# A pre-norm attention and FFN layer on one core: first weight columns in three groups, the next input split inside its step, another order in step 1

## The chip, the core and the metric

The kernel runs on one core of a Trainium2 chip. The metric is the device time of one execution in microseconds (us), lower is better. The kernel before was run three times.

## What is computed

x is 8 batches of 512 rows of 256, all fp32. Attention with 16 heads of 64 reads a layer norm followed by an RMS norm of x, and its projected output is added to x; an FFN (256 to 1024 to 256, GELU) with a per-row router weight reads a layer norm of that and is added too.

```python
def rms_norm(x, gamma):
    norm = jnp.maximum(jnp.linalg.norm(x, axis=-1, keepdims=True), eps)
    return x / norm * x.shape[-1] ** 0.5 * (gamma + 1.0)
qkv = rms_norm(layernorm(x), gamma) @ w_qkv      # 256 x 3072
attn = jax.nn.softmax((q * scale) @ k.T)         # 8 batches, 16 heads, 512 x 512
x = x + (attn @ v) @ w_out
out = gelu(xt @ w1 + b1) @ w2 + b2
x = x + out * jnp.sum(combine, axis=-1, keepdims=True)
```

## The kernel before

Every product keeps fp32 accuracy by a split: an operand is held as a rounded **high part** (fp32r) and a **low part** (the value less its high part), and `products` (L449) multiplies high by high, low by high and high by low, so each block of one output costs six matmuls (two halves of K by three terms). So every intermediate that TensorE (PE) will read again is read twice out of PSUM: once by ScalarE (ACT), which writes the high part, then by VectorE (DVE), which subtracts and writes the low part (`lo`, L925). Weights are staged in SBUF and split the same way; their low parts are made by GpSimd (POOL, L871) or VectorE.

The attention work is a hand-written software pipeline. A *unit* n is one pair of heads and one tile of 128 query rows; there are 256. A *step* holds units 2*step and 2*step+1, and 16 steps are one batch. In step s, PE does, in this order (L645 to L665):

1. the transposes of the probabilities of unit 2s-3 (`transpose_prob`, L476, into banks 4 and 5),
2. the scores of units 2s and 2s+1 (`scores`, L457),
3. the transposes of unit 2s-2 (banks 6 and 7),
4. "aux" blocks of place 1 (bank 4), the weighted values of step s-2 (`weighted_values`, L502, bank 5), and aux blocks of places 2 and 3 (banks 6 and 7).

Aux blocks are what `plan_aux` (L75) lays out: `xt` (the normalised input transposed, two blocks per batch), `q`, `k` and `v` products of the next heads, and `out` (the output projection). VectorE takes for each unit the row maxima out of PSUM (`row_max`, L993), ScalarE the exponentials (`exp`, L737), VectorE the inverse of the row sums (L1000), and POOL scales the probabilities (`normalise_prob`, L839). ScalarE and VectorE then make the high and low parts of the transposed probabilities (`transposed_hi`, L726; `transposed_lo`, L982). High and low parts of aux blocks of places 2 and 3 are made at the *start of the following step* (L773 and L1056). The exponentials write into three buffers `prob`, so unit n's may start only when unit n-3 has been transposed. At the very start `prob`, `wstage` and `halves_out` hold staged weights, so the first units also wait for these to be split (L742).

Steps -10 to -1 are the lead-in. SyncE issues the loads of x, then 128 columns each of the q and k weights (`first_stage`, L307), then six chunks of the remaining qkv weights (L281 to L286). Each chunk is split at a *slot* (half a step) of the table L301:

```python
POOL_CHUNKS = (0, 2, 3, 4, 5, 6, 7)
slot_of_chunks = {-12: [0], -9: [1], -8: [2], -6: [3], -5: [4], -4: [5], 6: [6], 10: [7]}
```

Until its operands are there PE runs matmuls on zeros (`keep_warm`, L640; counts in `WARM`, L58). The first batch's transposed input is made in steps -4 and -3, q and k of the first two heads in step -3, and step 0 starts with their scores. Later batches' `xt` blocks are issued at the end of step 13 of each batch (rel == 13, L95), in banks 6 and 7. PE's next transposes into these banks (unit 2s-2, L490) wait until both have their low parts.

## Time and profile before

| | us |
|---|---|
| median of 3 runs | 1218.33 |
| lowest, highest | 1218.26, 1219.44 |
| the profiled execution | 1219.89 |
| its span in the trace | 1218.0 |

The profiled execution's time has 1.9 us around its span. Times in the trace count from the span's start. Steps 0 to 127 lie between 19 and about 1000 us, with the FFN behind them.

### The profile page before, as it was taken

What the parts mean: (1) busy time and instruction counts of PE and PEld (TensorE: products, weight loads), DVE (VectorE), ACT (ScalarE), POOL (GpSimd) and SP (SyncE); (2) the same over time, 40 slices, a digit from 0 to 9 for tenths busy, and PEclk for the clock granted to TensorE, in tenths of its full rate; (3) what the DMA queues carried; (4) which work ended last, traced back from release to release, by engine and by line L of the source; (5) the groups of instructions that cost most, each with busy time, mean ns of one, the idle gap of its engine ahead of it and who ended that gap; (6) DMA issues with size and microseconds to landing.
All of it is one profiled execution on the core that took longest, in us unless ns stands there. A gap on an engine that the chain in (4) does not pass through costs nothing. (4 is left out here: it accounts for less than half of the span.)

```text
span 1218.0 us, 29275 instructions
## 1 busy us (share of the span) xinstructions
PE 1189.3 (98%) x11355; PEld 1041.3 (85%) x11355; DVE 962.4 (79%) x1739; ACT 894.0 (73%) x1926; POOL 640.3 (53%) x797
## 2 busy tenths in 40 slices
PE   7999999999999999999999999999999989999998
PEld 5878888888888888888888888888888878888887
DVE  5788788877887788878887897889788987666644
ACT  5788888888888888788878888888788884334432
POOL 5565555555565555556555565556555654322221
PEclk9999999999999999999999999999999999999999
DMA  4122111311131113111311131113111222111100
GB/s 158 36 53 71 36 36 37 87 36 36 36 88 36 37 36 87 36 37 36 88 36 36 37 87 37 36 36 87 36 36 36 71 77 85 35 48 57 36 18 36
DMA packets 32633, 62.92 MB, mean 52 GB/s; under 512 B 5744, under 2 KB 9072, under 8 KB 32496
## 3 DMA queue, kind: packets, MB, share of 16 engines
q1 hardware_dynamic: 32496, 61.05, 19.5%
q8 instruction: 92, 1.51, 0.5%
q14 instruction: 45, 0.37, 0.1%
HBM read 19.08 MB, written 8.39 MB: 23 GB/s over the span
## 5 line engine op out<-in xcount | busy, mean ns | idle before, releaser
L827 POOL TENSOR_SCALAR prob<-prob,rowinv 128x512 f32<-128x512 f32 x512 | 350.5, 699 | 313.3 <-DVE rowinv L1000 310.1
L744 ACT ACTIVATE prob<-ps,negmax 128x512 f32<-128x512 f32 x512 | 347.1, 686 | 36.8 <-DVE negmax L995 32.8
L927 DVE TENSOR_TENSOR pT_lo<-ps,pT_hi 128x512 fp32r<-128x512 f32 (+1 forms) x384 | 320.3, 862 | 24.9 <-ACT pT_hi L735 18.8
L995 DVE TENSOR_REDUCE negmax<-ps 128x2 f32<-128x1024 f32 x256 | 310.9, 1215 | 1.1 <-PE ps L473 1.1
L497 PEld LDWEIGHTS ps<-identity,prob 64*128 64x128 f32 x4096 | 154.0, 139 | 71.3 <-issue 33.4
L732 ACT ACTIVATE pT_hi<-ps 128x1024 fp32r<-128x1024 f32 x128 | 131.5, 1027 | 104.4 <-issue 101.5
L497 PE MATMUL ps<-identity,prob 64*128 64x64 f32 x4096 | 177.8, 226 | 13.0 <-POOL prob L827 10.2
L469 PE MATMUL ps<-nat 64*128 64x512 f32 x1024 | 171.7, 411 | 1.4 <-DVE nat L927 1.4
L511 PE MATMUL ps<-pT_hi,vbuf 128*128 128x256 f32 x1024 | 164.3, 282 | 3.0 <-DVE pT_lo L927 3.0
L511 PE MATMUL ps<-pT_lo,vbuf 128*128 128x256 f32 x1024 | 164.0, 282 | 0.0
L511 PEld LDWEIGHTS ps<-pT_hi,vbuf 128*128 128x128 f32 x1024 | 144.1, 189 | 9.9 <-DVE pT_lo L927 4.2
L735 ACT ACTIVATE pT_hi<-ps 128x512 fp32r<-128x512 f32 x256 | 140.5, 610 | 16.4 <-PE ps L497 16.4
L511 PEld LDWEIGHTS ps<-pT_lo,vbuf 128*128 128x128 f32 x1024 | 140.6, 190 | 0.0
L453 PE MATMUL ps<-xT_hi,wbig_hi 128*128 128x512 f32 x320 | 133.1, 416 | 2.4 <-DVE xT_lo L928 2.4
L847 POOL TENSOR_TENSOR att_hi_v<-att_hi_v,att_lo_v 128x512 f32<-128x512 f32 x64 | 83.4, 1302 | 91.6 <-DMA att_lo_v<-halves_out 91.6
L1000 DVE RECIPROCAL rowinv<-rowsum 128x2 f32<-128x2 f32 x256 | 40.9, 160 | 112.6 <-ACT prob L744 112.3
L453 PE MATMUL ps<-xT_hi,wbig_lo 128*128 128x512 f32 x320 | 127.5, 398 | 0.0
L453 PE MATMUL ps<-xT_lo,wbig_hi 128*128 128x512 f32 x320 | 125.5, 392 | 0.0
L744 ACT ACTIVATION_READ_ACCUMULATOR prob<-ps,negmax 128x1 f32 x512 | 102.9, 201 | 0.0
L473 PE MATMUL ps<-nat 64*128 64x512 f32 x512 | 102.0, 393 | 0.0
L469 PEld LDWEIGHTS ps<-nat 64*128 64x128 f32 x1024 | 88.1, 188 | 14.0 <-DVE nat L927 1.9
L836 POOL TENSOR_SCALAR pT_hi<-prob 128x512 fp32r<-128x512 f32 x64 | 41.0, 643 | 102.8 <-ACT prob L761 102.8
(116 smaller groups left out, 2317.0 us busy)
## 6 DMA issues: line engine op xcount, KB each, us to landing
att_hi_v<-halves_out SPq DMA_DIRECT2D x128, 128.0 KB, 2.3
att_lo_v<-halves_out SPq DMA_DIRECT2D x128, 128.0 KB, 2.4
xres<-in_x SPq DMA_DIRECT2D x8, 512.0 KB, 3.5
x_scratch<-xres SPq DMA_DIRECT2D x8, 512.0 KB, 2.9
out_y<-f_o SPq DMA_DIRECT2D x16, 256.0 KB, 2.0
xin<-in_x SPq DMA_DIRECT2D x7, 512.0 KB, 4.2
wstage<-in_w SPq DMA_DIRECT2D x4, 512.0 KB, 3.8
xin<-x_scratch SPq DMA_DIRECT2D x3, 512.0 KB, 3.8
```

What stands on the lines that cost most here:

```text
L453: ins = pe.matmul(dst, stationary[i], moving[j], start=first and n == 0, stop=last and n == len(terms) - 1)
L469: pe.matmul(ps[:, PS_SCORE[n % 2] + h, :], part[rows, q_part, q0:q0 + P], part[rows, k_part, :], start=q_part == QH, stop=False)
L473: pe.matmul(ps[:, PS_SCORE[n % 2] + h, :], part[rows, QH, q0:q0 + P], part[rows, KL, :], start=False, stop=True).then_inc(s_score, 1)
L497: ins = pe.transpose(ps[:, bank + r, a * DH:(a + 1) * DH], prob[rows, n % NPROB, a * P:(a + 1) * P], identity[rows, rows])
L511: ins = pe.matmul(ps[:, PS_OUT, h * 2 * P:(h + 1) * 2 * P], vbuf[:, quad % 2, k, pair % 2 * 2 + h, :], pT[part][:, t % 2, h * TT + k, :], ...
L732: act.activation(even_tile(n)[0], two_bank_blocks(PS_PT_EVEN), ACT.Copy).then_inc(s_pthi, 2)
L735: act.activation(odd_tiles(n)[r][0], bank_blocks(PS_PT_ODD + r), ACT.Copy).then_inc(s_pthi, 1)
L744: act.activation(prob[:, n % NPROB, j * SEQ:(j + 1) * SEQ], ps[:, PS_SCORE[n % 2] + j, :], ACT.Exp, bias=negmax[:, n % 4, j:j + 1], accum_ ...
L827: return pool.tensor_scalar(dst, src, scalar, 1.0, ALU.mult, ALU.mult)
L847: pool.tensor_tensor(att_hi_v[:, :], att_hi_v[:, :], att_lo_v[:, :], ALU.add).then_inc(s_head, 1)
L927: return dve.tensor_tensor(dst, full, hi, ALU.subtract)
L995: dve.tensor_reduce(negmax[:, n % 4, :], ps[:, PS_SCORE[n % 2]:PS_SCORE[n % 2] + 2, :], AX.X, ALU.max, negate=True).then_inc(s_max, 1)
```

## The change

**First columns in three groups.** Beside the 128 q and k columns of the first pair of heads (group 0), the same of the second pair (group 1) and 256 v columns (group 2) are loaded in pieces of their own, into `att_lo_v` and `xres`, ahead of the six chunks, which are 768 wide now. ScalarE makes the high parts of the three in slots -17 to -15, VectorE the low part of group 0, POOL those of groups 1 and 2 once the normalised input is there. The chunks are split later (0 and 1 behind the first input's high parts, 2 in step -2, 3, 4 and 5 in steps 0, 1 and 2), all low parts by POOL.

**Around the first products.** k comes before q; each half of K waits for its own half of the input. The first query tile (128 columns) has its high and low part made first, and unit 0's scores wait for it alone. `gain` is computed behind the normalisation. Three and one fewer matmuls on zeros. The second half of the first v block moves from step 1 to step 0 (place 4, bank 5).

**Step 1.** VectorE takes both row maxima and ScalarE the exponentials of unit 2 before unit 0's transposed parts.

**The next batch's input.** In step 13 of each batch ScalarE makes the high part of the first `xt` block inside the step, ahead of the second exponentials; for batches 1 to 7 VectorE makes the high part of the second block itself (`input_hi`) and then both low parts, at the end of the step. For the FFN's first input (behind batch 7) ScalarE makes both high parts there.

**POOL.** The layer norm's powers (`powers`) come behind `normalise_prob` of the odd unit instead of ahead of it.

The diff's core:

```diff
-WARM = {FIRST_STEP: 22, -3: 5}
+WARM = {FIRST_STEP: 19, -3: 4}
-PS_AUX = {1: 4, 2: 6, 3: 7}
+PS_AUX = {1: 4, 2: 6, 3: 7, 4: 5}
...
-            blocks += [(1, "q", 0), (2, "k", 0)]
+            blocks += [(1, "k", 0), (2, "q", 0)]
         if step == 0:
-            blocks.append((3, "v", 0, 0))
+            blocks += [(3, "v", 0, 0), (4, "v", 0, 1)]
...
-        POOL_CHUNKS = (0, 2, 3, 4, 5, 6, 7)
-        slot_of_chunks = {-12: [0], -9: [1], -8: [2], -6: [3], -5: [4], -4: [5], 6: [6], 10: [7]}
+        POOL_CHUNKS = (0, 1, 2, 3, 4, 5, 6, 7)
+        slot_of_chunks = {-6: [0, 1], -4: [2], 1: [3], 3: [4], 5: [5], 6: [6], 10: [7]}
...
+            for k in range(KT):
+                sp.dma_start(first_stage[1][:, k], first_source[1][:, k]).then_inc(s_first_load[1], 16)
+            for k in range(KT):
+                sp.dma_start(first_stage[2][:, k], first_source[2][:, k]).then_inc(s_first_load[2], 16)
             for i in range(7):
                 load_weight(sp, i)
...
+                if n == 0:
+                    pe.wait_ge(s_q_first, 1)
+                if n == 1:
+                    pe.wait_ge(s_aux, aux_index[("q", 0)] + 1)
...
+                if n == 1:
+                    pe.wait_ge(s_aux, aux_index[("v", 0, 1)] + 1)
...
+                    start = P if pair == 0 else 0
+                    if start:
+                        act.activation(nat[:, 0, QH, 0:start], bank[:, 0:start], ACT.Copy, scale=SCALE)\
+                            .then_inc(s_q_first_hi, 1)
+                        act.wait_ge(s_q_first, 1)
...
-                for block_of_aux in aux_of(step - 1)[1]:
+                for block_of_aux in late_blocks(step - 1):
                     aux_hi(*block_of_aux)
...
-                if 0 <= 2 * step - 2 < NUNIT:
+                if 0 <= 2 * step - 2 < NUNIT and step != 1:
                     transposed_hi(2 * step - 2)
                 if 0 <= 2 * step < NUNIT:
                     exp(2 * step)
+                if step == 1:
+                    transposed_hi(0)
...
                     copy_halves(step - 2)
+                for block_of_aux in turned_blocks(step):
+                    aux_hi(*block_of_aux)
                 if 0 <= 2 * step + 1 < NUNIT:
                     exp(2 * step + 1)
...
+            def input_hi(block_no, place, kind, b, k):
+                dve.wait_ge(s_auxfull, block_no + 1)
+                link(dve.tensor_scalar(xT[0][:, k, :], ps[:, aux_bank(block_no), :], gain[:, k:k + 1], None, ALU.mult))
...
                 slot_tasks(2 * step + 1)
+                for block_of_aux in turned_blocks(step):
+                    if split_by_vector(*block_of_aux[2:]):
+                        input_hi(*block_of_aux)
+                for block_of_aux in turned_blocks(step):
+                    aux_done(*block_of_aux)
```

**ScalarE at the start**, before (`wbig_hi` is the high part of the qkv weights, `xT_hi` that of the transposed input, `nat` holds q and k):

```order
L767 ACTIVATE wbig_hi<-att_hi_v 128x2x2x128 [waits first_columns_loaded]
L770 ACTIVATE wbig_hi<-prob 128x896 [waits weights_loaded0]
L770 ACTIVATE wbig_hi<-prob 128x896 [waits weights_loaded1]
L770 ACTIVATE wbig_hi<-prob 128x896 [waits weights_loaded2]
L703 ACTIVATE xT_hi<-ps,gain 128x512 [waits aux_block_in_psum] x2
L770 ACTIVATE wbig_hi<-wstage 128x896 [waits weights_loaded3]
L708 ACTIVATE nat<-ps 128x512 [waits aux_block_in_psum]
```

and now:

```order
L812 ACTIVATE wbig_hi<-att_hi_v 128x2x2x128 [waits first_columns_loaded0]
L812 ACTIVATE wbig_hi<-att_lo_v 128x2x2x128 [waits first_columns_loaded1]
L812 ACTIVATE wbig_hi<-xres 128x2x256 [waits first_columns_loaded2]
L740 ACTIVATE xT_hi<-ps,gain 128x512 [waits gain_ready,aux_block_in_psum] x2
L815 ACTIVATE wbig_hi<-prob 128x768 [waits weights_loaded0]
L815 ACTIVATE wbig_hi<-prob 128x768 [waits weights_loaded1]
L753 ACTIVATE nat<-ps 128x512 [waits aux_block_in_psum]
L747 ACTIVATE nat<-ps 128x128 [waits aux_block_in_psum]
L750 ACTIVATE nat<-ps 128x384 [waits first_query_tile_done]
```

The input's high parts stand ahead of every whole chunk, and behind the two small groups.

**ScalarE in steps 1 and 2** now (the first row is the exponential of unit 2, `halves_out` here stages chunk 4):

```order
L786 ACTIVATE prob,rowsum<-ps,negmax 128x512 [waits weights_lo_pool,rowmax_done]
L786 ACTIVATE prob,rowsum<-ps,negmax 128x512
L774 ACTIVATE pT_hi<-ps 128x8x128 [waits probabilities_transposed]
L786 ACTIVATE prob,rowsum<-ps,negmax 128x512 [waits probabilities_transposed,rowmax_done]
L786 ACTIVATE prob,rowsum<-ps,negmax 128x512
L815 ACTIVATE wbig_hi<-halves_out 128x768 [waits weights_loaded4]
L777 ACTIVATE pT_hi<-ps 128x8x64 [waits probabilities_transposed]
```

Before, `pT_hi` of unit 0 stood first, the v block's copies stood behind unit 3's exponentials, and no chunk was split here.

**VectorE where the input is turned** (steps 13 and 14 of a batch; `vbuf` is v, `xT_lo` the input's low part), before:

```order
L927 TENSOR_TENSOR vbuf<-ps,vbuf 128x2x128
L1000 RECIPROCAL rowinv<-rowsum 128x2 [waits exp_done]
L928 SCALAR_TENSOR_TENSOR xT_lo<-ps,gain,xT_hi 128x512 [waits aux_hi_done] x2
L927 TENSOR_TENSOR pT_lo<-ps,pT_hi 128x8x64 [waits pT_hi_done] x2
L995 TENSOR_REDUCE negmax<-ps 128x2 [waits scores_done]
```

and now:

```order
L982 TENSOR_TENSOR vbuf<-ps,vbuf 128x2x128
L1026 TENSOR_SCALAR xT_hi<-ps,gain 128x512 [waits aux_block_in_psum]
L983 SCALAR_TENSOR_TENSOR xT_lo<-ps,gain,xT_hi 128x512 [waits aux_hi_done,dve_step]
L983 SCALAR_TENSOR_TENSOR xT_lo<-ps,gain,xT_hi 128x512
L1063 RECIPROCAL rowinv<-rowsum 128x2 [waits exp_done]
L982 TENSOR_TENSOR pT_lo<-ps,pT_hi 128x8x64 [waits pT_hi_done] x2
L1058 TENSOR_REDUCE negmax<-ps 128x2 [waits scores_done]
```

The low parts pass the inverse of the odd unit's row sums, and one more operation stands ahead of them.

## Rows read from the trace of the kernel before

**Rows 1.** The page, part 1: busy time of each engine, its share, and instructions.
```profile
PE 1189.3 (98%) x11355; PEld 1041.3 (85%) x11355; DVE 962.4 (79%) x1739; ACT 894.0 (73%) x1926; POOL 640.3 (53%) x797
```

**Rows 2.** Windows, one per batch: length, engines busy us (count), PEclk, DMA share, GB/s.
```profile
246.37:369.27 122.90, 121.43 (x1253) 106.69 (x1254) 102.80 (x171) 99.50 (x226) 70.14 (x88) 1.00 0.20 49
...
sum 860.30, PE 851.86 PEld 749.29 DVE 721.68 ACT 702.12 POOL 495.20; mean PE 121.69 PEld 107.04 DVE 103.10 ACT 100.30 POOL 70.74
```

**Rows 3.** PE's waits: line, waited for, us in total, times, longest.
```profile
PE ps L497 <- POOL prob L827: 10.2, 14, 1.0
```

**Rows 4.** Timeline, start: start us, us, engine line op out<-in xcount [idle <-releaser].
```profile
5.98 0.63 ACT L767 ACTIVATE wbig_hi<-att_hi_v 128x512 fp32r<-128x512 f32 x1 [3.97 <-DMA att_hi_v<-in_w_qkv]
...
8.80 1.38 DVE L923 TENSOR_SCALAR xn<-xin,ln_mv,ln_scale 128x256 f32<-128x256 f32 x4
...
10.95 2.15 DVE L927 TENSOR_TENSOR wbig_lo<-prob,wbig_hi 128x896 fp32r<-128x896 f32 x1 [0.77 <-ACT wbig_hi L770]
...
11.96 1.25 ACT L703 ACTIVATE xT_hi<-ps,gain 128x512 fp32r<-128x512 f32 x2
...
13.02 1.40 DVE L928 SCALAR_TENSOR_TENSOR xT_lo<-ps,gain,xT_hi 128x512 fp32r<-128x512 f32 x2
...
14.52 0.47 PE L453 MATMUL ps<-xT_hi,wbig_hi 128*128 128x512 f32 x1 [2.37 <-DVE xT_lo L928]
...
16.19 0.60 ACT L708 ACTIVATE nat<-ps 128x512 fp32r<-128x512 f32 x1 [2.15 <-PE ps L453]
...
17.63 0.59 ACT L711 ACTIVATE nat<-ps 128x512 fp32r<-128x512 f32 x1
...
19.00 0.73 PE L469 MATMUL ps<-nat 64*128 64x512 f32 x4 [1.45 <-DVE nat L927]
```

**Rows 5.** Timeline, step 0 to the beginning of step 2.
```profile
20.04 2.36 DVE L995 TENSOR_REDUCE negmax<-ps 128x2 f32<-128x1024 f32 x2 [1.09 <-PE ps L473]
...
21.30 0.69 ACT L744 ACTIVATE prob<-ps,negmax 128x512 f32<-128x512 f32 x1 [2.13 <-DVE negmax L995]
...
26.71 0.71 PE L497 MATMUL ps<-identity,prob 64*128 64x64 f32 x16
...
29.93 0.39 PE L453 MATMUL ps<-wbig_hi,xT_hi 128*128 128x256 f32 x1 [2.50 <-DVE pT_lo L927]
...
32.32 1.11 PE L497 MATMUL ps<-identity,prob 64*128 64x64 f32 x16
...
33.20 1.04 PE L469 MATMUL ps<-nat 64*128 64x512 f32 x4
```

**Rows 6.** Windows of 1 us: one inside the stretch of the lower clock.
```profile
31.00:32.00 1.00, 1.00 (x7) 1.00 (x6) 0.08 (x2) 0.96 (x3) 0.83 (x2) 0.50 0.00 0
```

**Rows 7.** The page, part 5: two of ScalarE's groups.
```profile
L732 ACT ACTIVATE pT_hi<-ps 128x1024 fp32r<-128x1024 f32 x128 | 131.5, 1027 | 104.4 <-issue 101.5 <-PE ps L497 2.9
...
L735 ACT ACTIVATE pT_hi<-ps 128x512 fp32r<-128x512 f32 x256 | 140.5, 610 | 16.4 <-PE ps L497 16.4
```

**Rows 8.** Timeline, step 3.
```profile
41.51 1.10 ACT L735 ACTIVATE pT_hi<-ps 128x512 fp32r<-128x512 f32 x2
...
43.60 0.74 PE L511 MATMUL ps<-pT_hi,vbuf 128*128 128x256 f32 x4 [0.43 <-DVE pT_lo L927]
```

**Rows 9.** Timeline, end of the second batch: steps 29 and 30.
```profile
245.43 0.74 DVE L927 TENSOR_TENSOR vbuf<-ps,vbuf 128x256 fp32r<-128x256 f32 x2
...
247.06 1.27 ACT L703 ACTIVATE xT_hi<-ps,gain 128x512 fp32r<-128x512 f32 x2
...
247.47 1.36 POOL L827 TENSOR_SCALAR prob<-prob,rowinv 128x512 f32<-128x512 f32 x2 [0.50 <-DVE rowinv L1000]
...
247.79 1.41 DVE L928 SCALAR_TENSOR_TENSOR xT_lo<-ps,gain,xT_hi 128x512 fp32r<-128x512 f32 x2 [0.41 <-ACT xT_hi L703]
...
249.30 0.71 PE L497 MATMUL ps<-identity,prob 64*128 64x64 f32 x16 [0.88 <-POOL prob L827]
```

**Rows 10.** Timeline, VectorE in the second batch.
```profile
223.48 1.51 DVE L923 TENSOR_SCALAR xn<-xin,ln_mv,ln_scale 128x256 f32<-128x256 f32 x2
```

## What the change is expected to do

> **What bounds the kernel now.** I read the busy times first: TensorE is busy for 1189.3 of 1218.0 us [rows 1]. The reader is to see that only idle time of TensorE, or time at a lower clock, can be won. The windows by batch say where it isn't: in a whole batch of 122.90 us TensorE works 121.43, VectorE 102.80, ScalarE 99.50, and over seven batches TensorE is idle for 8.4 us in all [rows 2]. So a batch offers about 1.2 us. TensorE's waits name the rest: its largest item is 10.2 us of 14 waits of the transposes (L497), none above 1.0 [rows 3]. The trace puts them down to POOL, but at the end of a batch POOL has started the pair of tiles at 247.47 that is not the one waited for, while VectorE's low part of the turned input ends at 247.79 + 1.41 = 249.20 and TensorE goes on at 249.30 [rows 9]. So this wait is for the next batch's input, 0.88 us, once per batch. The timeline of the start shows the other idle time: TensorE waits 2.37 us before its first product, 1.45 us before the first scores [rows 4], and 2.50 us in step 1, after which the granted clock is at half (1.2 GHz) [rows 5, 6].
>
> Two places are then to be costed: the first 45 us, and the end of each batch. Durations are those of the profiled execution, 1219.89 us.
>
> **The start, up to the first scores.** The normalised input (8.80 us) is no sooner. ScalarE makes the input's high part at 11.96, because three weight chunks stand ahead; VectorE takes the low part at 13.02, behind a chunk's low part that ends at 13.10 [rows 4]. Both chunks are gone. The last tile is normalised at 8.80 + 1.38 = 10.18, so the first half is turned at about 10.5, where ScalarE now begins. VectorE follows ScalarE by 0.73 (247.06 to 247.79 [rows 9]) at 11.25, its first low part takes 0.7, and TensorE, which follows by 0.1, starts at 12.05 instead of 14.52. A block of six products then takes 1.67 until its copy starts, the next 1.44 more [rows 4]: k is copied at 13.7, q at 15.15 instead of 17.63.
>
> The last leg shrinks too. Now it is 19.00 - 17.63 = 1.37. No row has a copy of 128 columns. ScalarE needs 1027 ns for 1024 and 610 for 512 columns [rows 7], 0.81 ns a column; carried on, 0.30 us for 128. VectorE's lies between nothing saved (0.7) and the same ratio (0.3). I take 0.3, since its durations also go with the columns. With 0.15 between engines that is 0.75, so the scores start at 15.9: 3.1 us earlier. Bounds are 2.5 (no gain in the last leg) and 3.3.
>
> One new risk is the two small groups of weights, 512 KB ahead of the chunks, whose copies stand ahead of the input's on ScalarE. Group 0 was issued third and is copied at 5.98 [rows 4]. The two new ones are issued 2 us behind it and may land at 8 to 9.5, each needing 0.6; they must be done by 10.5. I cost them at nothing, and what they are late is lost one to one. Fewer matmuls on zeros cost nothing, since TensorE waits for the input behind them.
>
> **Steps 0 to 3.** The remaining q columns (0.5 + 0.55 us) hold unit 1's scores until about 17.0. Four blocks of 1.44 follow (the second v block is now among them), so unit 2's scores start at 23.5. The row maxima of units 2 and 3 (2.36 a pair [rows 5]) end at 26.9, the v block's low part at 27.6, and TensorE turns unit 1 at 27.7 instead of 32.32. It is idle ahead of that for about 2 us: this idle time is moved, not gone. From there ScalarE is last: the exponentials of unit 2 (two of 0.69 [rows 5]) from 25.7, unit 0's high part 1.03, unit 3's exponentials to 29.45, chunk 4 (768 columns by the same slope 0.82, of which 0.75 counts), unit 1's high part. VectorE takes its low part to 32.0, the row maximum of unit 4 to 33.2, unit 2's low part and unit 5's maximum to 35.5. ScalarE's exponentials of unit 5 end at 36.9, chunk 5 adds 0.75, a k copy 0.6, and unit 3's high part begins at 38.2 instead of 41.51. TensorE's weighted values follow 2.09 behind it [rows 8]: **3.3 us earlier** than 43.60. The two chunks split here cost 1.5 of that; POOL's share of them (nearly 2 us each) stands ahead of a pair of probabilities, but ends before these are due. Behind this point the order is the old one, and TensorE's lead should last.
>
> What half of the clock costs now: the twelve products of 256 columns from 29.93 to 32.32 take 2.39 for 1.44, the transposes 1.11 for 0.71, the next scores 1.04 for 0.73 [rows 4, 5]: 0.95 + 0.40 + 0.31 = 1.66 us.
>
> **The end of each batch.** ScalarE copied both halves at 247.06, behind the exponentials. Now the first stands ahead of them, at about 245.8 (two exponentials of 0.69 ahead of 247.06), and pushes them to 247.65. VectorE has made v's low part at 245.43 + 0.74 = 246.17 [rows 9] and was then nearly idle until 247.79; it copies the second half. No row has this operation; the low part of equal size, 0.7, is the nearest, and a plain copy could be somewhat less. Then both low parts: 246.9 + 1.41 = 248.3. TensorE must also wait for the pushed exponentials before unit 29's scores (247.75), and gets to its transposes at 248.65 instead of 249.30. I take **0.6 us** a batch, bounds 0 and 0.88; seven batches give 4.2. At the last turn, before the FFN, ScalarE copies both halves ahead of the exponentials: 0 to 0.6 lost, I take 0.2. POOL's powers behind the probabilities change no wait that the trace shows: 0.
>
> **The sum**: 1219.89 - 3.3 - 4.2 + 0.2 = 1212.6. The median of the runs is 1218.33, 1.56 below the profiled execution, nearly the 1.66 of the lower clock. I read that as most runs being without it. Their start then gains only 3.3 - 1.66 = 1.64, and 1218.33 - 1.64 - 4.0 = 1212.7. Both ways agree; I forecast 1212.6.
>
> **The rivals.**
> A. *The start's gain is given back*, 0.18. The clock falls in the new idle time before unit 1's transposes (2 us, less than the 2.50 that brought it down, about the 2.37 that did not), or the groups land late, or the chunks in steps 0 to 2 hold ScalarE longer. The price of a whole fall is 1.66, the start's net gain 1.64: 1214.3. The Trainium skill ("TensorE: Matmul & The Clock Gate", section "Why this matters for your kernels") warns only of idle gaps longer than any in this start. By that rule the clock would fall in neither kernel and this case's first cause would be void; the trace doesn't agree, since it fell after 2.50 us.
>
> B. *The batch ends gain nothing*, 0.12: VectorE's new copy runs while POOL scales probabilities, and is held up. The trace has such a case: the normalisation of two tiles took 1.51 us [rows 10], where four took 1.38 alone [rows 4]. Twice the 0.7 brings TensorE to 249.1, and the gain to 0.2 or less: 1216.7. The Trainium skill ("SBUF — State Buffer", section "Who interferes with whom") says that VectorE contends with GpSimd only when it reads two SBUF operands or runs in a two-port mode, and this copy reads PSUM. By the rule B does not happen and the sum stays at 1212.6; no run here shows it yet.
>
> C. *The median runs have the lower clock too*, and the 1.56 is something else: then all 3.3 counts against 1218.33: 1211.0. Chance 0.12.
>
> D. *Slower*: VectorE sets the pace behind each turn. The inverse of unit 27's row sums now waits for three operations of the turned input: from 247.2 to 248.4, 1.2 us. If VectorE, and not TensorE, were the engine that is behind, seven batches would lose up to 8.3 and the time be 1218.3 - 1.6 + 8.3 = 1225. It decides where VectorE's slack in the rest of a batch is below 1.2 us; it has 122.9 - 102.8 = 20 us [rows 2]. Chance 0.03.
>
> E. *Nothing of it reaches the end*, both gains absorbed by waits that this trace hides: 1218. Chance 0.05.
>
> **How the numbers follow.** My forecast has 0.50. I count 0.2% (2.4 us) as what a measurement can tell from no change. Forecast, A and C lie below 1215.9: 0.50 + 0.18 + 0.12, and a part of B makes 0.83 faster. The rest of B, and E, are the same: 0.14. D is slower: 0.03. The range must hold 0.8: from C's 1211.0, less 1 for a better last leg, to B's 1216.7, where A lies inside: 1210.0 to 1216.7.
>
> **What would show it.** In the new profile: the first product at about 12.1 and the first scores at 15.9; a wait of about 2 us before unit 1's transposes near 27.7; unit 3's high part about 38.2; at the end of each batch a wait of some 0.3 for the exponentials where 0.88 stood, with VectorE's copy at 0.7; PE's 10.2 us of waits at L497 down to about 6. I am wrong if the first product starts after 13, if the clock shows half behind 27 us, if VectorE's copy takes over 1 us, or if the wait at the batch ends stays near 0.9.

## The result: 0.75% faster, more than forecast

| | before | changed |
|---|---|---|
| median of the runs | 1218.88 (4 runs) | 1211.37 (4 runs) |
| lowest, highest | 1218.26, 1221.93 | 1210.09, 1212.92 |
| the profiled execution, its span | 1219.89, 1218.0 | 1211.50, 1209.7 |

The medians differ by 7.5 us; the ratio is 0.9925 [0.991, 0.9941], which is 9.1 us, with 7.2 to 11.0 as its interval. Forecast were 5.7 against the median of the runs and 7.3 against the profiled execution. Measured again later beside other kernels, the changed kernel stood at 1211.78 and the kernel before at 1222.46, ratio 0.9914 [0.9899, 0.9928].

The page's busy times of the changed kernel answer to [rows 1], TensorE's waits (line, waited for, us, times, longest) to [rows 3]:

```profile
PE 1189.3 (98%) x11351; PEld 1040.2 (86%) x11351; DVE 964.9 (80%) x1746; ACT 890.3 (74%) x1922; POOL 641.4 (53%) x800
```

```profile
PE ps L530 <- POOL prob L876: 3.6, 7, 1.0
PE ps L530 <- DVE vbuf L982: 3.0, 6, 2.1
```

TensorE is busy just as long; all that went is idle time, 28.7 us before and 20.4 now. The 10.2 us at the transposes that were put down to POOL are 3.6 (about 6 forecast). Of the 3.0 us that are now put down to VectorE's v block (`vbuf`), 2.05 are the idle time of step 1, which has moved here.

**The start.** Timeline of the changed kernel, start us, us, engine, operation, and in brackets the idle time before it, to be held against [rows 4, 5, 8]:

```profile
7.36 0.63 ACT L812 ACTIVATE wbig_hi<-att_lo_v 128x512 fp32r<-128x512 f32 x1 [0.84 <-DMA att_lo_v<-in_w_qkv]
8.37 1.38 DVE L978 TENSOR_SCALAR xn<-xin,ln_mv,ln_scale 128x256 f32<-128x256 f32 x4
8.62 0.63 ACT L812 ACTIVATE wbig_hi<-xres 128x512 fp32r<-128x512 f32 x1 [0.64 <-DMA xres<-in_w_qkv]
...
11.80 0.48 PE L479 MATMUL ps<-xT_hi,wbig_hi 128*128 128x512 f32 x1 [0.30 <-DVE xT_lo L983]
...
14.88 0.28 ACT L747 ACTIVATE nat<-ps 128x128 fp32r<-128x128 f32 x1 [0.80 <-PE ps L479]
15.19 0.29 DVE L983 SCALAR_TENSOR_TENSOR nat<-ps,nat 128x128 fp32r<-128x128 f32 x1 [0.38 <-ACT nat L747]
...
15.63 0.72 PE L499 MATMUL ps<-nat 64*128 64x512 f32 x4 [0.79 <-DVE nat L983]
...
27.58 0.94 PE L530 MATMUL ps<-identity,prob 64*128 64x64 f32 x16 [2.05 <-DVE vbuf L982]
...
38.37 1.10 ACT L777 ACTIVATE pT_hi<-ps 128x512 fp32r<-128x512 f32 x2
...
40.47 0.75 PE L544 MATMUL ps<-pT_hi,vbuf 128*128 128x256 f32 x4 [0.43 <-DVE pT_lo L982]
```

The reader is to see the path arrive where the sum put it: first product 11.80 (12.05 forecast), scores 15.63 (15.9), unit 1's transposes 27.58 with 2.05 us of idle time ahead (27.7, about 2), unit 3's high part 38.37 (38.2), weighted values 40.47 instead of 43.60 (40.3). Both new groups are in SBUF in time. But most of 0.43 of these 3.13 us is no gain of the change: the normalisation began at 8.37 instead of 8.80, 0.35 of it because the last of the input's statistics, which wait for the load, began at 4.59 instead of 4.94. The other 0.08 is `gain`, which now stands behind. And the low clock is still there, only earlier (windows of 1 us; the clock is the third figure from the end, as in [rows 6]):

```profile
27.00:28.00 1.00, 0.42 (x12) 0.45 (x13) 0.44 (x2) 1.00 (x4) 0.00 (x0) 0.94 0.56 142
28.00:29.00 1.00, 1.00 (x14) 0.97 (x13) 0.85 (x1) 1.00 (x4) 0.00 (x0) 0.50 0.86 312
30.00:31.00 1.00, 1.00 (x8) 0.49 (x5) 0.37 (x1) 1.00 (x3) 1.00 (x3) 0.50 0.00 0
31.00:32.00 1.00, 1.00 (x19) 0.93 (x18) 1.00 (x3) 0.16 (x2) 1.00 (x1) 0.85 0.00 0
```

It is 1.2 GHz from 27.9 to 31.3, which begins 0.3 us behind the 2.05 us of idle time; before it was so from 30.5 to 33.9.

**The turn of the batch.** The same place as [rows 9], in the changed kernel:

```profile
241.87 0.68 ACT L740 ACTIVATE xT_hi<-ps,gain 128x512 fp32r<-128x512 f32 x1
242.25 0.75 DVE L1026 TENSOR_SCALAR xT_hi<-ps,gain 128x512 fp32r<-128x512 f32 x1
...
243.03 1.41 DVE L983 SCALAR_TENSOR_TENSOR xT_lo<-ps,gain,xT_hi 128x512 fp32r<-128x512 f32 x2
...
244.75 0.65 PE L530 MATMUL ps<-identity,prob 64*128 64x64 f32 x16
```

VectorE's new copy takes 0.75 with POOL at work beside it (241.74 to 243.10), and TensorE's wait of 0.88 is gone. As a clock for the body of the kernel I use the starts of ScalarE's copies of transposed probabilities (`pT_hi`), two in a step. Around each of the seven turns three intervals differ: 6.43, 1.90 and 6.95 us before, 5.86, 1.75 and 6.92 now. Each turn gains **0.75 us**.

The sum by the traces: the start 3.12 (the first of these copies in step 5 comes at 55.55 instead of 58.67), turns 7 x 0.75 = 5.25, the last turn 0.2, less 0.33 that random stretches (below) took more in this execution than in the other: 8.2 of the 8.3 that the spans differ by.

### The profile page after: what moved, and what is told of

The parts are those of the page before. It is cut to its first block and busy times, and to the rows that moved or that the text cites. A ratio compares the mean times of both kernels' runs of the same rounds, so it can differ in the third digit from the quotient of the medians.

```text
span 1209.7 us, 29228 instructions
## 1 busy us (share of the span) xinstructions
PE 1189.3 (98%) x11351; PEld 1040.2 (86%) x11351; DVE 964.9 (80%) x1746; ACT 890.3 (74%) x1922; POOL 641.4 (53%) x800
## 5 line engine op out<-in xcount | busy, mean ns | idle before, releaser
L786 ACT ACTIVATE prob<-ps,negmax 128x512 f32<-128x512 f32 x512 | 347.1, 686 | 35.7 <-DVE negmax L1058 31.9
L530 PEld LDWEIGHTS ps<-identity,prob 64*128 64x128 f32 x4096 | 154.6, 139 | 64.7 <-issue 35.8
L777 ACT ACTIVATE pT_hi<-ps 128x512 fp32r<-128x512 f32 x256 | 140.5, 610 | 15.9 <-PE ps L530 15.9
```

Source lines behind the costliest of these rows:

```text
L530: ins = pe.transpose(ps[:, bank + r, a * DH:(a + 1) * DH], prob[rows, n % NPROB, a * P:(a + 1) * P], identity[rows, rows])
L777: act.activation(odd_tiles(n)[r][0], bank_blocks(PS_PT_ODD + r), ACT.Copy).then_inc(s_pthi, 1)
L786: act.activation(prob[:, n % NPROB, j * SEQ:(j + 1) * SEQ], ps[:, PS_SCORE[n % 2] + j, :], ACT.Exp, bias=negmax[:, n % 4, j:j + 1], accum_ ...
```

## The experiments

All ratios are against the kernel before, run on the same chip in the same set of runs. From set to set the kernel before's own median lay between 1218.9 and 1222.5, so where the medians of two changed kernels from different sets are compared, the difference is less sure than a ratio.

### The two parts apart

`batch_ends_alone` is the kernel before with `turned_blocks`, `split_by_vector` and `input_hi` added for steps from 0 on; `start_alone` is the changed kernel with

```diff
-            return [block for block in aux_of(step)[1] if block[2] == "xt"]
+            return [block for block in aux_of(step)[1] if block[2] == "xt" and step < 0]
...
-            return kind == "xt" and args[1] == KT - 1 and 1 <= args[0] < B
+            return False
```

> The kernel before, with one part of the change alone: the next batch's input is split within its step, the second block's high part by VectorE; the start is as before. Theory 1 (the parts add up, and the trace's own steps give their size): each of the seven batch ends gains 0.7 us and the end of the kernel 0.1, so the time is some 5.1 us below the kernel before, ratio 0.9958; in the trace the first transposes of the third batch come with no idle time from the input left before them. Theory 2 (the record's size of a batch end, 0.6 us, and 0.2 lost at the end): 4.0 us below, ratio 0.9967. Theory 3 (record's rival B, VectorE's copy gives it back): under 1 us below.

> The changed kernel with the batch ends undone: only the three groups of first columns, the first query tile's split and the order in step 1 are left. Theory 1 (the start's whole gain counts in the median, because the kernel before has its stretch of half clock in its ordinary executions too): 3.1 us below the kernel before, ratio 0.9974. Theory 2 (the record's reading: most executions of the kernel before have no such stretch, so only part of it counts): 1.6 us below, ratio 0.9987. In the trace unit 1's transposes begin near 27.6 us and unit 3's high part near 38.4 in both.

Measured: 1216.67, 0.9965 [0.9953, 0.9978], and 1218.41, 0.9976 [0.9963, 0.9988], the kernel before at 1221.94. So the batch ends give 4.3 us (interval 2.7 to 5.7, which holds both expectations), and the start 2.9 (1.5 to 4.5); together that is 0.9941, at the upper edge of the first comparison's interval. The turns read 5.85, 1.75 and 6.91 in the one trace and 6.42, 1.90 and 6.94 in the other, to 0.02 at every turn. Rival B is out. For the start the size is nearer Theory 1's 3.1 than the record's 1.6, but the interval just holds 1.6 too (0.9987): the time alone doesn't decide it, the clock below does.

### Whose gain is the turn

`after_scalar_takes_high` is the changed kernel with `split_by_vector` returning False: ScalarE makes both high parts, still within the step.

> The changed kernel, but both high parts of a turned block are ScalarE's, as in the kernel before; they are still taken within the step. Theory 1 (what gains at a batch end is the earlier place, and VectorE's high part only takes 0.7 us off ScalarE): ScalarE's exponentials of the step come 0.65 us later, so the turn gains little or nothing of its 0.72: 3 to 5 us above the changed kernel, near 1215. Theory 2 (the place alone carries the gain): within 0.5 us of the changed kernel. In the trace the wait of TensorE for the exponentials after a turn is 0.25 us plus 0.65 in the first case.

Measured: 1215.91, 0.9961 [0.9949, 0.9973], 4.1 us above the changed kernel's 1211.78 of another set, and as far above two kernels of its own set that keep VectorE's copy (1211.72 and 1211.65, next section and below). Its timeline at the second turn:

```profile
244.52 1.26 ACT L740 ACTIVATE xT_hi<-ps,gain 128x512 fp32r<-128x512 f32 x2
...
245.66 0.70 ACT L786 ACTIVATE prob<-ps,negmax 128x512 f32<-128x512 f32 x1
...
247.17 0.74 PE L499 MATMUL ps<-nat 64*128 64x512 f32 x4 [0.63 <-ACT prob L786]
```

The exponentials are pushed back by the second copy, and unit 29's scores wait 0.63 us for them. The turn reads 6.42, 1.76, 6.91: only 0.19 of the 0.75 comes from the earlier place, 0.56 from giving one copy to VectorE on top of it. VectorE's copy without the earlier place wasn't measured.

### The start's parts

`after_old_step1_order`: maxima and exponentials no longer ahead of unit 0's copies in step 1 (`and step != 1` and the two moved calls undone). `after_whole_first_tile`: the first query tile undivided (`start = 0`). `groups_alone`: both of these and the old batch ends. `order_alone`: the kernel before with the new order of step 1 alone.

> The changed kernel with the old order in step 1: unit 0's transposed probabilities are copied before the maxima and exponentials of units 2 and 3. Theory 1 (the order matters because unit 1's normalisation and the copies of units 2 and 3 hang on it): the weighted values of units 0 and 1 begin 0.5 to 1.3 us later than 40.5 and the time is that much above the changed kernel. Theory 2 (the order is worth nothing, the columns' groups carry the start's whole gain): within 0.3 us of the changed kernel.

> The changed kernel without the split of the first query tile: the copies of 512 columns are one piece again, so the first scores wait for all four blocks. Theory 1: the first scores move from 15.6 to 16.0 us and the time by 0.3 to 0.4 us. Theory 2 (ScalarE's chain from the first exponentials to unit 3's high part has slack there): level, within 0.2 us.

> The start's first part alone: the first columns in three groups, on their new engines, with the old order in step 1, the undivided first query tile and the old batch ends. Theory 1 (the first product comes 2.7 us sooner, but the old order in step 1 hands most of it back, as unit 1's transposes then wait 4.4 us for VectorE's value block): the weighted values of units 0 and 1 come at most 0.8 us sooner than before, ratio 0.9990 to 1.0000. Theory 2 (the groups carry the gain and the order is a detail): ratio 0.9980 or below.

> The kernel before with the order in step 1 alone: maxima and exponentials of units 2 and 3 ahead of unit 0's copies, nothing else. Theory 1 (start gain = groups x order: each is worth little without the other): unit 1's transposes begin near 29 us instead of 29.93, 0.3 to 1.5 us below the kernel before. Theory 2 (the order is worth its whole 2 us by itself, because TensorE's idle time before unit 1's transposes is what it shortens): 1.8 to 2.5 us below.

Measured: 1214.40, 0.9953 [0.9938, 0.9967]; 1211.72, 0.9935 [0.9922, 0.9947]; 1220.58, 0.9984 [0.9974, 0.9995]; 1224.20, 1.0015 [1.0004, 1.0025]. With the groups there, the order is worth some 2.7 us (1214.40 against 1211.72 and 1211.65 in the same set), though its six executions scatter from 1211.33 to 1217.01. Alone it costs 1.8 us, which neither theory had. The groups alone give 2.0, where I had expected at most 1.2; the interval (0.6 to 3.2) holds both theories' numbers. The divided first tile can't be told from nothing. The timeline of `after_old_step1_order` shows what the order is for:

```profile
29.97 1.12 PE L530 MATMUL ps<-identity,prob 64*128 64x64 f32 x16 [4.43 <-DVE vbuf L980]
```

4.43 us of idle time where the changed kernel has 2.05. Both first products come at 11.8, and the weighted values at 42.73 instead of 40.47, 2.3 us later. (The profiled execution is the quickest of the six all the same, since its random stretches, below, are the smallest of all traces, 2.6 us.)

What makes the order slower alone shows in `order_alone`'s timeline:

```profile
34.90 0.58 PE L453 MATMUL ps<-wbig_hi,xT_hi 128*128 128x256 f32 x1 [4.05 <-DVE pT_lo L929]
```

In the kernel before, the second v block stands in step 1 and waits until unit 0's low part has freed its bank, 2.50 us of idle time [rows 5]. The new order puts that low part behind both maxima, and the wait grows to 4.05. The change moves this block to step 0, so order and block belong together. How much of the 1.8 us this wait is and how much the clock isn't settled: the trace has the low clock from 13.2 to 20.0 and again from about 33.7 to 40.5, and the eleven executions have a mean clock of 0.997 or 0.994 where the kernel before has 0.999 too.

### The low clock

`before_gap_filled` and `after_gap_filled` put matmuls into a bank that nobody reads at the idle time of step 1 (ten and eight); `before_both_gaps_filled` also has seven more warming ones ahead of the first products.

```diff
+            def fill_gap(count):
+                for n in range(count):
+                    pe.matmul(ps[:, 4, :], wqkv[0][:, 0, 0:P], xT[0][:, 0, :], start=True, stop=True)
...
+                if step == 1:
+                    fill_gap(10)
```

> The kernel before with ten idle matmuls into a bank of PSUM that nobody reads, issued in step 1 in the gap that ends near 30 us, so that TensorE has no long idle stretch there. If the half clock from 30.75 to 34.16 us costs what the record said (1.66 us) and stands in every execution of the kernel before, this one is 1.0 to 1.7 us below it (some of the ten matmuls may delay the transposes by up to 0.5). If the ordinary executions of the kernel before are without the half clock, it is level or up to 0.5 us above it. In the trace the granted clock of 31 to 34 us is then 1.0.

> The changed kernel with eight idle matmuls into a bank of PSUM that nobody reads, issued in step 1 in the gap that ends near 27.6 us. The changed kernel's profile has the half clock from 27.9 to 31.3 us. If that stretch is on the path: 1.0 to 1.6 us below the changed kernel's median, so near 1210. If ScalarE's chain covers it (weight chunks and exponentials set the next steps): level with the changed kernel, within 0.4 us, so 1211 to 1211.7.

> The kernel before with ten idle matmuls in the gap of step 1 (as in before_gap_filled) and twelve warming matmuls instead of five ahead of the first products. Theory 1 (most executions of the kernel before have the half clock twice, and that is 1.5 to 3 us of their time): no half clock in the profile or only one beside idle time, mean clock 0.999 or more in most executions, 1 to 2.5 us below the kernel before, ratio 0.998 to 0.9992. Theory 2 (the clock goes along with late loads but costs little by itself): the clock is full, the time within 0.5 us of the kernel before.

Measured: 1221.10, 0.9991 [0.9978, 1.0004]; 1211.99, 0.9927 [0.9914, 0.994]; 1221.00, 1.0002 [0.9988, 1.0016]. The stretch of step 1 is gone in all three traces, as this window of `before_gap_filled` shows:

```profile
31.00:32.00 1.00, 1.00 (x6) 0.67 (x4) 1.00 (x1) 1.00 (x4) 0.00 (x0) 1.00 0.00 0
```

Yet no median moved by more than its interval. The intervals are wide: for the old start they run from 0.5 us slower to 2.7 faster and from 1.9 slower to 1.5 faster, so a gain of 1 us could hide in them. The traces measure more finely. From the first product to one of ScalarE's copies in step 5 (at 58.67 us in the kernel before) passes, in the traces that have the whole old or the whole new start:

| traces with | low clock in step 1 | us |
|---|---|---|
| old start | none (two traces, filled) | 43.12, 43.10 |
| old start | 30.5 to 33.9; 31.7 to 35.1 | 44.15, 44.19 |
| old start, and low over the first products | 32.1 to 35.5; 33.4 to 36.8 | 45.65, 45.65 |
| new start | none (three traces) | 43.62, 43.62, 43.58 |
| new start | 27.9 to 31.3; 28.8 to 32.2; 29.1 to 32.5 | 43.75, 43.90, 44.02 |
| new start | about 29 to 35.7 (two); 30.8 to 37.7 | 45.64, 45.60, 45.60 |

The price goes by where the stretch lies: 1.05 us in the old start, 0.13 to 0.40 in the new one, 2.0 where it lasts to 35.7 or beyond. Some pairs aren't clean: both filled traces of the old start have their first product over 1 us later than the others (next section), and one of the traces in each of the two dearest rows (`before_gpsimd_waits`, `after_gpsimd_free`) differs from its neighbours in a wait of POOL. `after_whole_first_tile` has the stretch from 30.1 to 33.5, and 44.89; how much of that is the clock and how much the undivided tile, which brings its first scores 4.54 us behind the first product instead of 3.83, isn't separated.

The mean granted clock of every execution says how common the stretch is. The full clock all through would read 1.000, a single stretch of 3.4 us in a span of 1218 reads 0.999. None of 90 executions of the kernel before in these sets reads 1.000; four of the twelve of `before_both_gaps_filled` do, and three of the eleven of `start_alone`.

### GpSimd beside VectorE at the start

The traces of the old start differ in something larger. `before_look` is the kernel before again; `before_gpsimd_waits` makes POOL's first weight chunk wait for the normalised input; `after_gpsimd_free` takes that wait out of the changed kernel.

```diff
-                    pool.wait_ge(s_xn_first, TT)
                     for g in (1, 2):
```

> The kernel before itself, for one more profile of its start. Theory 1 (VectorE and GpSimd meet when the first chunk of weights lands early against the normalisation): if GpSimd begins more than 0.5 us before the normalisation's usual end, that takes about 3.1 us, otherwise 1.38. Theory 2 (independent of each other): no such pairing.

> The kernel before with one wait more: GpSimd's first low part of a weight chunk (128x896) waits until the first input is normalised. Theory 1 (in many executions of the kernel before the two meet, VectorE's normalisation takes 3.1 us instead of 1.4 and the half clock comes a second time): the normalisation is 1.38 us in the profile and the median is 1 to 2.5 us below the kernel before, ratio 0.998 to 0.9992. Theory 2 (the landing of the loads alone makes the kernel before slower than its profile): level, within 0.5 us.

> The changed kernel without GpSimd's wait for the normalised input ahead of its two groups of first columns; the groups' data is there at 7.4 and 8.6 us. Theory 1 (GpSimd beside VectorE's normalisation holds it up): GpSimd subtracts from about 8.0 on, VectorE's normalisation of 1.38 us becomes 2.0 to 3.2, and the time is 0.7 to 2 us above the changed kernel. Theory 2 (no contention worth a number): level, within 0.3 us.

Measured: 1222.98 (one execution); 1221.49, 0.9997 [0.9988, 1.0006]; 1214.86, 0.9947 [0.9931, 0.9962]. Timeline of `before_gap_filled` (the row at 9.97 is the third of the four tiles at 9.33, shown by itself in a narrower window):

```profile
9.33 3.18 DVE L929 TENSOR_SCALAR xn<-xin,ln_mv,ln_scale 128x256 f32<-128x256 f32 x4
...
9.95 2.08 POOL L877 TENSOR_TENSOR wbig_lo<-prob,wbig_hi 128x896 fp32r<-128x896 f32 x1 [1.54 <-ACT wbig_hi L776]
...
9.97 2.21 DVE L929 TENSOR_SCALAR xn<-xin,ln_mv,ln_scale 128x256 f32<-128x256 f32 x1
...
12.43 2.97 DVE L933 TENSOR_TENSOR wbig_lo<-prob,wbig_hi 128x896 fp32r<-128x896 f32 x1
...
16.82 0.47 PE L453 MATMUL ps<-xT_hi,wbig_hi 128*128 128x512 f32 x1 [0.83 <-DVE xT_lo L934]
```

and of `after_gpsimd_free`:

```profile
8.15 1.27 POOL L909 TENSOR_TENSOR wbig_lo<-att_lo_v,wbig_hi 128x512 fp32r<-128x512 f32 x1 [0.29 <-ACT wbig_hi L812]
...
8.51 0.93 DVE L973 SCALAR_TENSOR_TENSOR ln_scale<-ln_pow,ln_norm 128x4 f32<-128x4 f32 x1
...
9.47 2.33 DVE L977 TENSOR_SCALAR xn<-xin,ln_mv,ln_scale 128x256 f32<-128x256 f32 x4
9.97 1.36 POOL L909 TENSOR_TENSOR wbig_lo<-xres,wbig_hi 128x512 fp32r<-128x512 f32 x1 [0.55 <-ACT wbig_hi L812]
```

Four normalisations take 1.38 us alone and 3.14 to 3.18 with POOL's subtraction beside them, in three of seven traces of the old start. One tile bears all of it: a tile takes 0.41, but the one that starts while POOL's subtraction is under way takes 2.21 and ends at 12.18, 0.15 behind POOL's end at 12.03. So in these rows VectorE doesn't run slower, it stands until POOL is through. VectorE's own subtraction of 896 columns does the same: it takes from 1.96 to 3.00 us (2.15 in [rows 4], 2.97 here), and in all seven traces it ends 0.94 or 0.95 us behind the end of one of POOL's. No trace has it alone.

From the normalisation's start to the first product pass 5.72 us in the recorded profile, and 5.76, 5.90, 5.95, 7.48, 7.49 and 7.86 in the others. In eleven traces of the new start it is 3.42 or 3.43 (3.72 in `groups_alone`, which has the low clock there). `after_gpsimd_free` has 4.38. POOL's two subtractions hold VectorE up twice, `ln_scale` for 0.93 instead of 0.16 and the normalisation for 2.33 instead of 1.38, 1.7 us in all. By the medians the kernel is 3.1 us slower than the changed one (another set); in the trace the rest is the low clock from 30.8 to 37.7, but two kernels that have the wait show a stretch as long, so the wait isn't shown to cause it. So POOL's wait is worth its place.

In the old start the wait alone gives nothing that can be told from noise (0.7 us slower to 1.5 faster): the normalisation is 1.38, but POOL then starts ahead of VectorE's own subtraction, which takes 2.90 and ends at 13.41 where the kernel before has 13.10. Theory 1's gain didn't come.

### The random stretches

A copy that usually comes 1.77 us behind the last one now and then comes up to 2.8 us behind it, always the one behind a merge of attention halves, 2.6 to 6.7 us an execution. The changed kernel at one such place:

```profile
595.90 0.61 SPq L418 DMA_DIRECT2D att_lo_v<-halves_out  x1
596.56 0.58 SPq L433 DMA_DIRECT2D xin<-in_x  x1
...
600.24 1.29 POOL L896 TENSOR_TENSOR att_hi_v<-att_hi_v,att_lo_v 128x512 f32<-128x512 f32 x1 [3.16 <-DMA att_lo_v<-halves_out]
...
603.59 2.70 POOL L876 TENSOR_SCALAR prob<-prob,rowinv 128x512 f32<-128x512 f32 x4
605.01 0.71 PE L530 MATMUL ps<-identity,prob 64*128 64x64 f32 x16 [0.57 <-POOL prob L876]
```

POOL waits for a load that lands 4.3 us after its issue instead of 2.3, the probabilities queue behind it, and TensorE waits for them. What makes the load late stays open. Here the next input (512 KB) is issued 0.66 us behind it, but of the seven loads of this trace that have 512 KB of x issued that close behind them five land in 2.3 to 2.4 us, and of the others eight take over 3.5. `after_attention_later` puts the merge behind the even unit's normalisation for three pairs of four, `after_attention_two_pairs` for two (`pair % 4 < 2`, the diff below), and `after_two_pairs_filled` adds the eight idle matmuls.

```diff
-                if step % 2 == 0 and 0 <= step // 2 - 2 < NPAIR:
+                attention_due = step % 2 == 0 and 0 <= step // 2 - 2 < NPAIR
+                if attention_due and (step // 2 - 2) % 4 >= 2:
                     attention_out(step // 2 - 2)
                 if 0 <= 2 * step < NUNIT:
                     normalise_prob(2 * step)
+                if attention_due and (step // 2 - 2) % 4 < 2:
+                    attention_out(step // 2 - 2)
```

> The changed kernel itself, beside the others of this set. The first comparison gave a ratio of 0.9925 [0.991, 0.9941]; the parts measured singly multiply to 0.9965 x 0.9976 = 0.9941. Theory 1 (the parts add, and the rest of the first ratio is what single executions differ by): 0.993 to 0.994. Theory 2 (the parts help one another): 0.9925 again or below. In its profile each turn of a batch takes 5.85 us between the copies of the transposed probabilities where the kernel before takes 6.43.

> The changed kernel with one more move, in GpSimd's queue: the merge of a pair's attention halves, which waits for a DMA, stands behind the normalisation of the even unit instead of ahead of it, for three pairs of four (not the one whose output products come in the next step). In the profiles so far a step now and then takes 2.0 to 2.7 us where 1.77 is usual, at the units behind that merge, 2.8 us of it in the kernel before and 3.1 in the changed one. Theory 1 (those steps are the DMA's late landing, handed on by GpSimd's queue): they vanish for three pairs of four, 1.5 to 2.5 us below the changed kernel, and the times scatter less. Theory 2 (something else stretches those steps): level with the changed kernel, or above it by up to 1 us because the odd unit's normalisation comes later.

> The changed kernel with the merge of the attention halves behind the even unit's normalisation for the first two pairs of each four alone, so that the fourth pair's load is issued as early as before. Theory 1 (what after_attention_later lost was the fourth pair's load, 0.37 us at each of seven places, and what it gained were the random stretches): those seven waits are gone, half of the random stretches stay, 0.5 to 1.5 us below the changed kernel. Theory 2 (the move costs what it gains wherever it is made, as the next pair's load comes later each time): level or above.

> The version of after_attention_two_pairs (1210.15, ratio 0.9909) with eight idle matmuls in step 1. In its executions with the half clock (1210.4, 1211.1) it was some 0.9 us above those without (1209.8). Theory 1 (the half clock in step 1 costs about 1 us where it falls): all executions near 1209.8, ratio 0.9905. Theory 2 (ScalarE's chain covers it): level with after_attention_two_pairs.

Measured: 1211.78, 0.9914; 1214.03, 0.9928 [0.9913, 0.9942]; 1210.15, 0.9909 [0.9894, 0.9924]; 1210.13, 0.9916 [0.9901, 0.9931]. POOL's wait for that load (us, times, longest), in the changed kernel, then with three pairs and with two pairs moved:

```profile
POOL att_hi_v L896 <- DMA att_lo_v<-halves_out: 80.8, 60, 3.2
```

```profile
POOL att_hi_v L896 <- DMA att_lo_v<-halves_out: 18.2, 16, 2.6
```

```profile
POOL att_hi_v L896 <- DMA att_lo_v<-halves_out: 44.4, 31, 2.7
```

The changed kernel's second measurement lies below the 0.993 to 0.994 that the parts measured singly had led me to expect. Nothing in the traces joins start and turn, and the intervals of the parts are wide; I leave it open.

With three pairs moved the stretches at the moved pairs are nearly gone, but each fourth pair's load is issued later and its copy comes 0.37 us or more late every time: the time is 2.3 us above the changed kernel's. With two pairs moved that is avoided, and the stretches add up to 3.0 us where they were 4.4 (kernels without the move have from 2.6 to 6.7, so one trace doesn't show the gain). The time is 1.6 us below the changed kernel's. Nine executions of these two versions (1209.66 to 1211.10) against nine of the changed kernel (1210.09 to 1212.92) make a gain likely, but they were not in one set, and the ratios' intervals overlap: it isn't shown. By their medians these are the fastest kernels here. The fill adds nothing.

`after_chunks_early_v` takes weight chunks 3 to 5 ahead of step 1's exponentials, and the v block's low part between the two maxima.

> The changed kernel with two more moves in the start: ScalarE takes the weight chunks 3, 4 and 5 before the exponentials of step 1 instead of between and behind them, and VectorE takes the second value block's low part between the maxima of units 2 and 3. Theory 1 (ScalarE's queue is what carries the start, from the exponentials of unit 2 to the weighted values): the 0.86 us of a chunk leave the chain once or twice, 0.9 to 1.7 us below the changed kernel, near 1210, and TensorE's idle time before unit 1's transposes is shorter than 2.05 us. Theory 2 (something else, TensorE at half clock or VectorE, takes the place): within 0.3 us of the changed kernel.

Measured: 1211.65, 0.9931 [0.9919, 0.9943]: nothing gained. TensorE's idle time before unit 1's transposes fell from 2.05 to 0.92 us, as Theory 1 had it, but unit 3's part of the path is as late as before (weighted values 28.70 us behind the first product, 28.67 in the changed kernel). So ScalarE's queue alone doesn't carry the start, which the record had assumed for both chunks (1.5 us).

## Why the prediction fell short

Two terms carry the miss. The start was counted at 1.64 us where 2.9 were measured, because of one wrong step, and the turns at 4.0 where the traces show 5.45, the last one included. The rest of the way from 5.7 to 9.1 us lies inside the interval (7.2 to 11.0).

- **The first product and the scores**: right. Net of the earlier input, the first product came at 12.2 (12.05 forecast). The copies of 128 columns took 0.28 and 0.29, where 0.30 was carried on from longer ones.
- **Steps 0 to 3**: right within 0.2 us in the profile, though the filled and the moved-chunk kernels show that the single legs were not as tight as the sum had them. Net of the input the start gained 2.7, not 3.3.
- **"I read that as most runs being without it"**: this step failed, and with it the 1.66 us taken off the start. No execution profiled with the old start and an unfilled gap is without the low clock, four of the five have it twice, and none of the 90 mean clocks reads 1.000. So the 1.56 us between the median of three runs and the profiled execution wasn't the low clock; I take it for scatter.

  Over these 90 executions of the kernel before in the later sets the mean granted clock goes with the time: 17 at 0.999 average 1219.9 us, 34 at 0.997 average 1222.3, 5 at 0.994 average 1225.6. The full clock comes with the quick executions but is mostly not what makes them quick, as the filled kernels show. Against the medians the start counts in full, 2.9 us where 1.64 was taken, and more where VectorE and POOL meet, which the recorded profile didn't show: it is the earliest first product of seven. The copy in step 5 that came at 58.67 there comes between 59.69 and 60.85 in the five other traces in which start and order are the old ones, and between 55.44 and 57.55 in eight of the whole new start, 3.6 us earlier on average. Rival C (1211.0) was the right reading, with 0.12. That its number is so close to 1211.37 is partly luck: its 3.3 us for the start are too much for the recorded profile, its 4.0 for the turns too little.
- **"What half of the clock costs": 1.66 us.** The low stretch's price at the old place measured 1.05 in the traces; the tally of slower matmuls was right in each row, and I read the other 0.6 as taken up by ScalarE's queue behind them, which no run separates.
- **Rival A**: the clock did fall again, behind idle time of 2.05 us. The record's reading that 2.37 us hadn't brought it down held for that one execution: the other six traces of the old start all have a low stretch somewhere between 11 and 20 us. The Trainium skill ("TensorE: Matmul & The Clock Gate", section "Why this matters for your kernels") warns only of longer gaps than this one; the trace again doesn't agree. Its price was wrong: 0.13 to 0.40 where the stretch is short, not 1.66, which I put down to ScalarE's chain above it, and 2.0 where it is long.
- **The turn, "0.6 us a batch"**: right mechanism, under-sized: 0.75. 0.56 come from VectorE's copy, 0.19 from the place, part of it one step later, where I had looked no further than the transposes. The exponentials were pushed and TensorE waited for them, as written, but for less: VectorE's low parts ended early enough to leave no wait at 244.75.
- **The last turn**: 0.2 lost was forecast, 0.2 gained: two intervals went from 1.90 to 1.79 and from 5.55 to 5.45.
- **Rival B**: VectorE's copy took 0.75 beside POOL. The Trainium skill ("SBUF — State Buffer", section "Who interferes with whom") says that an operation of VectorE with at most one input in SBUF, outside the two-port modes, doesn't contend with GpSimd; this copy's input is in PSUM, and the trace agrees. It also says that in a two-port mode the two do contend, and that the one that comes second stands for the whole of the other's instruction: the tile of 2.21 us at the start agrees with it, and this, not the turn, was where it mattered. The case that the rival rested on, 1.51 us for two tiles [rows 10], has its input in SBUF and not in PSUM. Rivals D and E: no sign.

Open: why the kernel before's medians range from 1218.9 to 1222.5 over six sets while the changed kernel stays at 1211.4 and 1211.8 in its two. The meeting of VectorE and POOL (up to 2.1 us at the first product) and the second low stretch (1.5 us where it lies over the products) are of that size, but neither, taken away alone, moved the median beyond intervals of 1 to 2 us either way, and no run takes both away at once.

## What to carry to other kernels

A single profile is one draw. Before a difference between it and the median is read as a mechanism, the same kernel should be profiled again, above all where loads land during the start. A low stretch of the clock is priced by what waits behind it, not by the matmuls in it. And when an operand has two readers or two equal halves, giving one half to the engine that has nothing to do just then was worth three times the earlier place in the queue here. An order that is worth 2.7 us behind one change cost 1.8 without it, so parts of a change are best measured both alone and taken out of the whole.

## What was unexpected of the hardware

- VectorE's normalisation SBUF to SBUF, 1.38 us for four tiles, takes 3.14 to 3.18 when a GpSimd subtraction begins ahead of one of the tiles: that tile stands until GpSimd is through (2.21 instead of 0.41). The two take turns: VectorE's subtraction of 128x896 ends 0.94 or 0.95 behind GpSimd's in seven traces, whatever it takes (1.96 to 3.00), and GpSimd's next one takes 2.7 to 2.9 instead of 2.1 where VectorE's lies ahead of it. In the recorded trace of the kernel before GpSimd began 0.30 us before the normalisation's end, but behind the last tile's start, and nothing was lost. VectorE's copy out of PSUM, 0.75, ran beside GpSimd without a wait.
- With the same program up to there and the same 2.05 us of idle time, the low clock stood from 27.9 to 31.3 in one execution (the changed kernel), from 28.9 to 35.8 in another (`after_scalar_takes_high`) and not at all in a third (`after_attention_two_pairs`, 2.0 us). Which of them comes isn't to be read from the kernel.
- Small loads (128 KB) that land in 2.3 us as a median take 3 to 4.3 now and then, with or without a large load behind them, and through one in-order queue that reaches TensorE several operations away.
